# A list of expert tiles told in two parts: 35 tiles from the first six chunks' counts, 40 at the end

## What is computed

```python
x = _layernorm(x + _L0_attn_ref(x, ...))        # time mixing, scan over time, channel mixing
xf = x.reshape(-1, Dm)
ys = _geglu(xf @ Ws1 + bs1) @ Ws2 + bs2         # shared expert, hidden 256
logits = (xf @ Wr + br) / TAU
top_val, top_idx = jax.lax.top_k(logits, 2)     # two of E = 12 experts
top_w = jax.nn.softmax(top_val, axis=-1)
h = jnp.einsum('nd,edh->enh', xf, We1) + be1[:, None, :]
yE = jnp.einsum('enh,ehd->end', _geglu(h), We2) + be2[:, None, :]    # hidden 384
x = _layernorm(x + ys + jnp.einsum('end,ne->nd', yE, w))
```

## Time and profile before

| | us |
|---|---|
| median of 3 runs | 450.01 |
| lowest and highest of them | 448.95 and 451.0 |
| span of the profiled execution | 471.4 |
| stretch from the last first-half product to the loop's first full tile | about 277 to 281 |
| end of the loop in the profiled execution | about 440 |

### The profile page before, as it was taken

The page is one execution under the profiler, slowest core; times in us unless marked ns, Lnnn a source line. Parts: engine busy times, 40 slices in busy tenths (PEclk is TensorE's granted clock), DMA queues, the critical chain, the costliest instruction groups (busy, mean ns, idle before and its releaser), DMA issues.

```text
span 471.4 us, 9935 instructions
## 1 busy us (share of the span) xinstructions
PE 399.7 (85%) x2503; PEld 307.2 (65%) x2503; DVE 312.4 (66%) x1065; ACT 295.7 (63%) x715; POOL 256.0 (54%) x328
## 2 busy tenths in 40 slices
PE   0566799998978988988593799999999999999991
PEld 0224466756746564664240369999999999999830
DVE  3799989999997997724560345656666665666162
ACT  2586699989796865663310237677777776777055
POOL 5666747567567857875566004444444444444264
PEclk9978799999999999997977699999999999999997
DMA  5389700000003000110122257876777776763394
GB/s 152 90 192 375 231 1 0 2 1 1 2 6 108 32 19 31 41 49 24 48 66 65 79 176 252 286 248 245 259 249 259 241 261 237 261 230 126 102 333 124
DMA packets 51471, 64.86 MB, mean 138 GB/s; under 512 B 8924, under 2 KB 35292, under 8 KB 51416
## 3 DMA queue, kind: packets, MB, share of 16 engines
q1 hardware_dynamic: 46968, 54.85, 35.1%
q0 software_dynamic: 4448, 9.38, 6.1%
HBM read 21.65 MB, written 13.91 MB: 75 GB/s over the span
## 4 chain that ended last, share of the span: by engine, by line
PE 51%; DVE 20%; issue 8%; SPq 6%; ACT 5%; POOL 4%; DMA 2%; another core or an unknown queue 2%; DVEq 0%; ACTq 0%; POOLq 0%
PE bank L1280 21%; PE bank L1298 11%; PE bank L987 4%; DVE rec L555 3%; DVE bst L475 2%; PE bank L969 2%; SPq L1087 2%; SPq L1086 2%; ACT z L690 2%; PE bank L1272 2%; PE bank L998 2%; PE bank L999 1%; PE bank L920 1%; POOL frs L821 1%
## 5 line engine op out<-in xcount | busy, mean ns | idle before, releaser
L1141 POOL DMA_INDIRECT routed_rows<-yo,goes_to x75 | 71.8, 957 | 112.8 <-DVE yo L1190 110.4
L1280 PE MATMUL bank<-xT,w 128*128 128x128 f32 x900 | 113.3, 276 | 0.6 <-ACT xT L1228 0.4
L1280 PEld LDWEIGHTS bank<-xT,w 128*128 128x128 f32 x900 | 106.6, 192 | 1.1 <-ACT xT L1228 0.5
L1182 DVE SCALAR_TENSOR_TENSOR actT<-bank,tile_bias,gl 128x128 f32<-128x128 f32 x225 | 65.3, 345 | 24.8 <-ACT gl L1234 15.1
L403 POOL DMA_INDIRECT dispatched_rows<-rows_all,slot_i x64 | 63.4, 990 | 22.7 <-issue 17.4
L1234 ACT ACTIVATE gl<-bank,tile_bias 128x128 f32<-128x128 f32 x225 | 65.9, 364 | 14.1 <-PE bank L1280 7.6
L1298 PE MATMUL bank<-we_sb,actT 128*128 x450 | 62.9, 276 | 1.0 <-DVE yo L1190 1.0
L1298 PEld LDWEIGHTS bank<-we_sb,actT 128*128 128x128 f32 x450 | 56.1, 192 | 1.6 <-issue 1.4
L1190 DVE SCALAR_TENSOR_TENSOR yo<-bank,goes,wb 128x128 f32<-128x128 f32 x75 | 26.3, 350 | 37.5 <-PE bank L1298 34.5
L1228 ACT ACTIVATE xT<-bank 128x128 f32<-128x128 f32 x75 | 20.8, 277 | 26.2 <-PE bank L1272 24.2
L969 PE MATMUL bank<-xk,wfk_sb 128*128 128x512 f32 x64 | 33.0, 626 | 4.9 <-DVE xk L572 3.8
(11 more groups left out here) (201 smaller groups left out, 778.4 us busy)
## 6 DMA issues: line engine op xcount, KB each, us to landing
w<-we_sb SPq DMA_DIRECT2D x75, 384.0 KB
x_all<-dispatched_rows SPq DMA_DIRECT2D x75, 68.0 KB
we_sb<-we SPq DMA_DIRECT2D x1, 4608.0 KB
rows_all<-x SPq DMA_DIRECT2D x8, 256.0 KB, 2.9
x_all<-routed_rows SPq DMA_DIRECT2D x8, 256.0 KB, 4.9
rows_all<-routed_rows SPq DMA_DIRECT2D x8, 256.0 KB, 5.3
out<-x_all SPq DMA_DIRECT2D x8, 256.0 KB, 2.5
routed_rows<-yo,goes_to POOLq DMA_INDIRECT x75
```

The source lines that it names most:

```text
L1141: ng.indirect_dma_start(routed, bass.IndirectOffsetOnAxis(ap=goes_to[n // U % DB][:, n % U:n % U + 1], axis=0), yo[n % YO][:, :], None).th ...
L1182: nv.scalar_tensor_tensor(actT[n % UA][:, at], ps_a[j][:, 0:P], tile_bias[:, j, n:n + 1], gl[n % 2][:, at], ALU.add, ALU.mult).then_inc(s2 ...
L1280: return nt.matmul(to[:, 0:P], w1[m][:, off:off + P], xT[m][:, :], start=True, stop=True)
```

## The change

Six of the eight chunks (three of the four routing batches, 48 of 64 scatters) are enough to know 35 tiles for certain: of 48 x 128 rows at least that many full tiles exist, whatever the routing. The list of tiles is now told in two parts, `LISTS` = (0, 35) and (35, 75).

- DVE: `find_tiles(0)` and the new `leave_tiles` stand behind `placed(2)`, `tell_tiles(0)` behind `logits(6)`. `find_tiles(1)` and `tell_tiles(1)` stand where the old ones stood and list what the first part left. `tell_tiles` now also copies the biases; ACT's `take_biases` is gone.
- PE: `tell(0)` behind `router(6)` and `tell(1)` in the place of `tell_words`; each does the words, the codes and the biases for its part. `tell_biases` ahead of `shared_back(7)` is gone.
- SP: weights of five tiles as soon as the first list is told, rows of ten tiles once 48 scatters have landed. The 12 pads are placed in the loop, one behind every second tile's rows. Ahead of the rows of tile 35 SP waits for the second list, the other 16 scatters and the pads.
- POOL: eight of the last batch's scatters ahead of the loop, the other eight in it, one ahead of the outputs of tiles 0, 2, ... 14. `deviation(7, "3")` stands two scatters later.

The number of tiles, the loop's body for each and the work behind the loop are unchanged.

```diff
+    LATE = BATCH[-1][0] * CT * K
+    AHEAD = -(-(LATE * P - E * (P - 1)) // P) // U * U
+    LISTS = ((0, AHEAD), (AHEAD, TILES))
+    PRELOOP = LATE + CT * K
...
+            def leave_tiles():
+
+                tiled_by(nv.tensor_scalar(capped[:, :, :], edge_of[:, 0:2, :], float(AHEAD), None, ALU.min))
+                tiled_by(nv.tensor_tensor(taken[:, 0:E], capped[:, 1, 0:E], capped[:, 0, 0:E], ALU.subtract))
+                tiled_by(nv.tensor_tensor(from_tile[:, :], base_tile[:, :], taken[:, 0:E], ALU.add))
                 nv.memset(owner[:, :], 0.0)
                 for m in range(SPAN):
                     last = nv.memset(places[:, m:m + 1], float(2 ** (BITS * m)))
                 tiled_by(last)
...
+            shared_act(1, 0); placed(v, 2, pT[:, PT_PREFIX]); find_tiles(0); leave_tiles(); x3(7); shared_act(1, 1); stats3(7)
+            shared_take(0); logits(6); tell_tiles(0); shared_act(2, 0); shared_act(2, 1); logits(7); chosen(v, 3)
             shared_take(1); shared_act(3, 0); shared_act(3, 1); placed(v, 3, pT[:, PT_PREFIX])
-            find_tiles(); shared_act(4, 0); shared_act(4, 1); shared_take(2); tell_tiles(); shared_take(3); shared_act(5, 0)
+            find_tiles(1); shared_act(4, 0); shared_act(4, 1); shared_take(2); tell_tiles(1); shared_take(3); shared_act(5, 0)
...
-            scatter_rows(g, 28, 29); deviation(6, "3"); scatter_rows(g, 29, 36); deviation(7, "3")
-            scatter_rows(g, 36, 64)
+            scatter_rows(g, 28, 29); deviation(6, "3"); scatter_rows(g, 29, 38); deviation(7, "3")
+            scatter_rows(g, 38, PRELOOP)
...
+            def tell(late):
+                lo, hi = LISTS[late]
+                n = hi - lo
+                t.wait_ge(s2["code_ready"], late + 1)
+                take_bank("pT", "bias_ready", late + 1)
+                nt.matmul(ps_tell[0:1, 0:n], word_at[:, late:late + 1], of_expert[:, lo:hi], start=True, stop=True)
+                nt.matmul(ps_tell[0:1, n:2 * n], low_p[0:EX, 0:1], of_expert[:, lo:hi], start=True, stop=True)
+                nt.matmul(ps_tell[:, 2 * n:3 * n], code_b[:, :], of_expert[:, lo:hi], start=True, stop=True)
                 for j in range(H1 // P):
+                    last = nt.matmul(ps_tell[:, (3 + j) * n:(4 + j) * n], be1_sb[:, j * P:(j + 1) * P], of_expert[0:E, lo:hi],
                                      start=True, stop=True)
                 last.then_inc(s2["bias_psum"], 1)
...
+            shared_up(1, 1); turn3(6); shared_gate(2, 0); router(6); tell(0); shared_gate(2, 1); shared_up(2, 0)
...
-            shared_up(7, 0); shared_back(6); shared_up(7, 1); tell_biases(); shared_back(7)
+            shared_up(7, 0); shared_back(6); shared_up(7, 1); shared_back(7)
...
-            sp.wait_ge(s["dispatched"], SLOTS // P * 16)
-            sp.wait_ge(s2["pads_placed"], E * 16)
+            sp.wait_ge(s["dispatched"], LATE * 16)
             for n in range(U):
                 load_rows(n, word_of(n))
             owners = {}
             for n in range(U, TILES + U):
                 if n >= 2 * U:
                     load_weights(n - U, owners.pop(n - U))
+                if n == AHEAD:
+                    sp.wait_ge(s2["tiles_known"], 2)
+                    sp.wait_ge(s["dispatched_late"], (SLOTS // P - LATE) * 16)
+                    sp.wait_ge(s2["pads_placed"], E * 16)
...
+                if n >= 2 * U and n % 2 == 0 and (n - 2 * U) // 2 < E:
+                    place_pad((n - 2 * U) // 2)
```

More of the change, by code:

```diff
@@ L148, in build @@
         gsh, ash = below_p, below_m
+        run_i = sb("run_i", [P, E], I32)
+        run_t = sb("run_t", [P, E], I32)
+        run_f = sb("run_f", [P, E])
+        pad_at = sb("pad_at", [1, E], I32)
+        edge_of = sb("edge_of", [P, 3, EX])
+        first, cumt, origin = edge_of[:, 0, :], edge_of[:, 1, :], edge_of[:, 2, :]
+        edge_on = sb("edge_on", [EX, 3, EX])
+        edge_at = sb("edge_at", [EX, 3])
+        capped = sb("capped", [P, 2, EX])
+        taken = sb("taken", [P, EX])
+        from_tile = sb("from_tile", [P, E])
+        word_at = sb("word_at", [EX, 2])
+        word = sb("word", [1, TILES], I32)
+        own_code = sb("own_code", [P, TILES])
+        owner = sb("owner", [1, TILES + U])
+        GROUPS = TILES // U
+        BITS = (E - 1).bit_length()
+        SPAN = U + 1
+        assert SPAN * BITS <= 24
+        places = sb("places", [1, SPAN])
+        owner_at = sb("owner_at", [1, GROUPS, SPAN])
+        packed_f = sb("packed_f", [1, GROUPS])
+        packed = sb("packed", [1, GROUPS], I32)
         block_buffers = ExitStack()
@@ L1082, in experts_sync, with place_pad @@
             sp.dma_start(be2_all[:, :], be2.rearrange("e c -> (e c)").partition_broadcast(P)).then_inc(s2["bias_spread"], 16)
-            sp.wait_ge(s2["rows_known"], 1)
-            for n in range(E):
+            def place_pad(n):
+                if n == 0:
+                    sp.wait_ge(s2["rows_known"], 1)
                 to = sp.value_load(pad_at[0:1, n:n + 1], min_val=0, max_val=E * REGION - P)
```

121 lines of the change are left out of this document (47 added, 74 removed).

## The result

The changed kernel takes **458.99 us** (median of 6 runs, 456.15 to 459.98) where the kernel before, timed beside it, takes 450.15 (6 runs, 448.95 to 451.13): a ratio of 1.0187, 95% interval 1.0162 to 1.0211. It is 1.9% slower; 446.0 was forecast, and the range ended at 451.5.

The account below looks back on a forecast made before the run. Rows for the first tiles were taken to arrive later than PE's shared expert, holding the loop's start to 259.5. Starting at 254.8 gains 4.7 us, less 0.7 for SP: 4.0 us faster, 446.0 us, range 438 to 451.5.

Parts of the forecast that it names:

- The rebuilt paths of before: Ahead of the loop, without stalls: PE done at 248.5, first rows issued at 250.8, full pace at 257.5 before clock loss.
- the first rival: Ahead of the loop: stalls partly remain in timed runs, on the row path; gain 10 us, 440 us; chance 0.17.
- the second: Rival ahead of the loop: PE path already equal, its extra 3.15 us eat the gain; about 450.5 us; chance 0.22.
- The clock term of before: At the old loop start: PE's idle wait for rows lowers the clock, costing 2 us (bounds 0 and 3.3).
- The agreement called the main reason: Loop start: rebuilt start 21.5 us before the trace's matches the 21.4 between profiled and timed runs, so rows come later.
- PE's price: PE ahead of the loop: wait 1.45 plus small products 1.95 less 0.25 saved, 3.15 us.
- The 254.8: Loop start after the change: full pace at 254.8, with PE done at 251.7 and rows already there.
- I take no clock loss here: PE behind tell(0)'s wait: no clock loss, since full-pace products followed a 2.26 us wait elsewhere.
- a half clock after it: Sign of being wrong, in the changed profile: half clock on PE behind the wait in tell(0).
- SP in the loop: First 25 tiles: 12 pads leave SP 4.4 us behind, 3.0 certainly free; 0.7 us taken (bounds 0 and 3).
- the third rival: Weight loads of tiles 10 to 30, behind pads: SP bounds the loop, 13 us lost or more, 459; chance 0.13.
- the mild pad of 1.7 us: Milder form of SP bounding the loop: a 1.7 us pad loses 4 to 7 us, 449 to 453 after the gain.

Follow-up runs that it names:

- e0: The kernel before, unchanged, profiled once more without the stalls of its first profile: 449.99 us (1 run), span 448.2 us.
- e12: Changed kernel with every pad of the loop issued twice, the second time to a place nothing reads: 477.55 us, ratio to before 1.0625.
- e2: Changed kernel with all 64 scatters ahead of the loop, the 12 pads staying in it: 459.58 us, ratio to before 1.0183.
- e1: Changed kernel with all 12 pads issued ahead of the loop, eight scatters staying in it: 453.11 us, ratio to before 1.0052.
- e3: Changed kernel with all pads and all 64 scatters ahead of the loop: 452.60 us, ratio to before 1.0044.
- e4: Changed kernel with scatters and pads ahead in the old order (pads, weights, rows after all scatters), list still in two parts: 453.68 us, ratio to before 1.0081.
- e5: Changed kernel with six pads ahead of the loop and six in it, one every fourth tile: 450.23 us, ratio to before 0.9995.
- e11: Changed kernel with all pads ahead of the loop, timed again unchanged on another chip: 452.44 us, ratio to before 1.0020.
- e15: Changed kernel with pads ahead of the loop and tell(1) one gate product later, tell(0) left early: 450.14 us, ratio to before 1.0011.
- e6: Changed kernel with pads ahead of the loop and tell(0) moved behind two large shared products: 446.38 us, ratio to before 0.9912.
- e7: Changed kernel with pads ahead of the loop and both tells cut into parts between large products: 448.53 us, ratio to before 0.9958.
- e9: Changed kernel with only tell(0) moved behind two large shared products, pads staying in the loop: 454.54 us, ratio to before 1.0102.
- e10: Changed kernel with pads ahead, tell(0) behind two large products, and an added PE wait for code_ready behind router(6): 446.42 us, ratio to before 0.9916.
- e13: Changed kernel with pads ahead, tell(0) behind two large products, and one unused semaphore more: span 443.5 us.
- e16: Changed kernel with pads ahead, tell(0) behind two large products and tell(1) one gate product later: 446.20 us, ratio to before 0.9928.
- e14: The kernel before with one unused semaphore more: span 446.8 us.

## Why the prediction was wrong, by its own steps

**In short:** 13.0 us lie between the forecast of 446.0 and the median of 458.99. SP's list in the loop has 6.2 of them (6.9 us for 0.7), the start 3.2 (a gain of 1.5 us for 4.7), a second portion of the clock's drop 1.7, and the stretch behind the loop 1.9.

**The rebuilt paths of before** were right at their ends, with errors on the way that cancelled (e0). The stalls were not in the timed runs, so the first rival falls, and with PE idle for 4.84 us the second does too. The Trainium skill, "Runtime: NRT & Kernel Launch", section "The ~15µs preamble/postamble breakdown", has a profile's total 6.2 us above the reported time. The two quantities of this case lie the other way round: in all runs the time is 1.7 to 1.8 us above the trace's span. Whether that span is what the page calls the total no run here shows.

**The clock term of before (2 us)** failed. The clock fell to a half as the text said, but that costs 0.3 to 0.8 us at the loop's start and not 2 (e0): the 6.7 us between the first rows and full pace came from a trace at full clock and were spent waiting for rows, and the slow clock runs beside that same wait. It had seemed to be confirmed since it brought the shift to the 21.4 us asked for. But those compared a span (471.4) with a time (450.0). With the 1.8 us between the two, 23.2 were to be explained, and the 23.6 without the term fit. The agreement called the main reason was a slip in the units of comparison. Without the term the start gains 257.5 - 254.8 = 2.7 us and not 4.7; measured from `router(6)` it is 1.5.

**PE's price (3.15 us)** was right in its parts: the wait was 1.28 us for 1.45, the small records took 2.0 us (210.49 to 212.46) for 1.95 (the 1.48 us for 12 records that the text reads in the earlier trace rows is 1.56 there). From `router(6)` to `back(7)` PE takes 36.85 us in e0 and 41.82 after; of these 5.0 us more the drop is 1.7, and 3.3 are left for the 3.15. That the loop started at 254.84 for 254.8 is luck nonetheless. The 254.8 is for the up product of tile 1, which comes some 0.7 us later than the gate product at 254.84. And `router(6)` came 2.5 us earlier than the 210.7 of the text, which hid the 1.7 us of the drop. "I take no clock loss here" failed. It rested on one row of the first half, a wait of 2.26 us with full products behind it. Here the wait had the router's 8 records ahead and 18 records of 12 or 13 rows behind, and the clock fell to a half for 1.7 us' worth at least, 5.1 at most. The text named "a half clock after it" among the signs of being wrong, and gave it no term. By the start column, the early tell costs 46.7 - 43.8 = 2.9 to 50.1 - 43.8 = 6.3 us.

**SP in the loop (0.7 us, bounds 0 and 3)** was the largest miss: 7.0 to 8.1 us. The mechanism and its place were those of the third rival, with a chance of 0.13. The size that failed is what SP falls behind: 4.4 us in the sum, 11.4 measured. By the 62.3 us for 24 tiles and 12 pads a pad costs (62.3 - 24 x 1.7) / 12 = 1.8 us in the loop (1.7 in the periods shown) and not 1.27, above the 1.37 from which the rival said that it decides; that is some 6 of the 7 us, and 1.70 for 1.67 us a tile is the rest. The 1.27 was that of a row of pads alone, where SP's register load for the pad's place takes 0.27 us (chain of the kernel before):

```profile
261.19 0.27 SPq L1086
```

Between other transfers it takes 0.76 us in the chain above and 0.39 to 0.76 in that of e12, mostly over 0.5. Why it takes longer there isn't known. The Trainium skill, "Runtime: NRT & Kernel Launch", section "Instruction fetch mechanics", gives some 0.2 us a register for the loads of this kind that the runtime adds. The 0.27 is near that, the 0.76 is not. The slack was not what failed: it is 4.5 to 4.7 us, within the 3 to 5.6 of the rival and above the 3.7 that the sum used (4.4 - 0.7). But it was taken from the weights, PE's need, and the rows are needed first. DVE's first step on a group waits for the rows of all five tiles. Its timeline in the profile after, the first of four such waits:

```profile
282.82 0.17 DVE L1178 TENSOR_TENSOR other<-x_all,own_code 128x5 f32<-128x5 f32 x1 [1.90 <-DMA x_all<-dispatched_rows]
```

The same step came every 10.6 us without a wait in e0. For the mild pad of 1.7 us the rival had given a loss of 4 to 7 us, which holds; its 449 to 453 was short by the gain at the start, which was 1.5 us or less for 4.7, and by the end.

**What had no step:** the 1.87 us behind the loop, 1.35 of them behind ACT's last work.

**The sum again,** with what was measured: 450.15 - 1.5 (start, one drop in it) + 6.9 (loop) + 1.9 (end) = 457.4 us. With a second drop of 1.7 it is 459.1, with a third 460.8. The median is 458.99, so a typical execution of the changed kernel has two. That is worked out, not seen: only the one execution has a trace, and it has one drop and a first stretch 1.07 us shorter (456.3; it took 456.15). But e2, with the same loop, was profiled in an execution with two portions, and that one took 459.67.

## What to carry to other kernels

Work that is moved into a loop "beside" others must be costed on its queue's own list, with its time measured between its new neighbours and not in a row of its like, and the slack must be taken from the first consumer of whatever is queued behind it. Here one instruction group per two tiles was too much, and one per four was free as long as the slack lasted. Small products on TensorE should stand where nobody has to wait for them: moving them behind two large ones turned 1.9% slower (with the pads ahead of the loop as well) into 0.9% faster. And a span is compared with a span, a time with a time.

## What the runs showed of the hardware that was not expected

- The granted clock falls to half (2.4 to 1.2 GHz) behind a wait of only 1.28 us that has nothing but small products around it, in each of the nine traces with it (after, e1 to e5, e11, e12, e15), in portions worth 1.7 us, one to three of them; without the wait there in none of six (e6, e7, e9, e10, e13, e16). A wait of 4.84 us in e0 lowered it as well. The Trainium skill, "TensorE: Matmul & The Clock Gate", "Part 1: The HAM clock gate (the "warmup" mystery)", has the clock follow how busy the array has recently been; the traces agree in kind.
- The same register load on SP takes 0.27 us in a row of pads (before, L1086) and 0.76 us between other transfers (after, L1097), where that is more than the issue of the pad's transfer itself (0.59).
- A half clock for some 3.4 us' worth behind 4.84 us of idle time cost only 0.3 us in e0 and 0.8 in e14, as the next work waited for rows anyway.
- A program's end can differ by 1.35 us between two kernels with the same last work (6.4 us in three traces, 7.7 in 17), and no row tells why.
